# A selective scan turned round: states on the partitions instead of channels, in a four-block kernel on one core

## The reference

```
def _L1_attn_ref(x, ...):                     # Mamba: d_inner = 256, n_state = 16, CHUNK = 32
    ...
    delta = jax.nn.softplus(dlt @ W_dt.T + b_dt)          # per token and channel
    A = -jnp.exp(A_log)                                   # per channel and state
    dA = jnp.exp(jnp.einsum('bld,dn->bldn', delta, A))
    dBu = jnp.einsum('bld,bln,bld->bldn', delta, Bm, u)
    ...
    def step(carry, inp):
        a, bu, c = inp
        carry = a * carry + bu
        y = jnp.einsum('bkdn,bkn->bkd', carry, c)         # sum over the 16 states
        return (carry, y)
    ...                                                   # started anew every 32 tokens
    y = y * jax.nn.silu(res)
    return y @ W_out.T + b_out
```

## Time and profile before

| what | us |
|---|---|
| median of 3 runs | 1242.27 (1234.53 to 1244.73) |
| the profiled execution | 1238.27 |
| its span | 1236.5 |
| PE busy, of the span | 1003.6 |
| DVE busy | 819.9 |
| POOL busy | 725.4 |
| ACT busy | 656.3 |

### The profile page before, as it was taken

One profiled execution on the slowest core, in us unless ns is written; L12 is line 12 of the kernel. 1 busy time (PEld: TensorE's weight loads), 2 busy tenths in 40 slices (PEclk: granted clock), 3 DMA queues, 4 the chain that ended last, 5 costly groups with the idle time before them and its releaser, 6 DMA issues.

```text
span 1236.5 us, 11304 instructions
## 1 busy us (share of the span) xinstructions
PE 1003.6 (81%) x3604; PEld 500.5 (40%) x3604; DVE 819.9 (66%) x1473; ACT 656.3 (53%) x1020; POOL 725.4 (59%) x572
## 2 busy tenths in 40 slices
PE   0455889789989999879998999879887976977785
PEld 0233535335535544444544535434333332332231
DVE  1412231585766786578879886898688789789751
ACT  1133465665675667756686656665624643553231
POOL 0012133757667747675877677776866786787422
PEclk9866788788878899889899988989978987897996
DMA  4000200453434524254552554545554665576420
GB/s 110 0 9 1 77 1 21 160 194 113 179 104 153 206 113 153 68 206 152 205 181 104 212 192 150 180 173 176 205 186 190 205 225 179 198 254 213 144 103 17
DMA packets 55715, 176.60 MB, mean 143 GB/s; under 512 B 7332, under 2 KB 17896, under 8 KB 51560
## 3 DMA queue, kind: packets, MB, share of 16 engines
q1 hardware_dynamic: 55656, 175.89, 41.0%
HBM read 172.99 MB, written 2.88 MB: 142 GB/s over the span
## 4 chain that ended last, share of the span: by engine, by line
PE 50%; DVE 19%; POOL 12%; ACT 10%; issue 4%; DMA 3%; SPq 2%; POOLq 0%; DVEq 0%; ACTq 0%
PE yp L1366 12%; DVE hs L899 5%; PE mp L1261 4%; PE pp L1298 4%; POOL dbu L638 4%; PE fp L1165 4%; PE mp L1271 4%; PE fp L1173 3%; DMA bcast<-held 3%; PE fp L1179 3%; DVE hs L906 2%; ACT L928 2%; PE mp L1277 2%; SPq L379 2%; PE pp L1230 2%
## 5 line engine op out<-in xcount | busy, mean ns | idle before, releaser
L638 POOL TENSOR_TENSOR dbu<-du,bcast 128x1024 f32<-128x1024 f32 x128 | 341.0, 2667 | 142.4 <-DMA bcast<-held 74.4
L899 DVE TENSOR_TENSOR_SCAN hs<-dA,dbu 128x512 f32<-128x512 f32 x256 | 300.4, 1206 | 58.7 <-POOL dbu L638 18.1
L1366 PE MATMUL yp<-hs,ident 128*128 128x512 f32 x512 | 294.9, 709 | 38.6 <-DVE hs L906 26.7
L1121 ACT ACTIVATE dA<-delta,mA 128x496 f32<-128x496 f32 x256 | 169.4, 672 | 145.2 <-DVE hs L899 142.0
L1366 PEld LDWEIGHTS yp<-hs,ident 128*128 128x128 f32 x512 | 107.0, 224 | 179.1 <-issue 110.7
L906 DVE TENSOR_TENSOR hs<-hs,bcast 128x1024 f32<-128x1024 f32 x96 | 156.9, 1634 | 2.9
L836 DVE SCALAR_TENSOR_TENSOR he<-mp,vectors,he 128x512 f32<-128x512 f32 x128 | 89.8, 741 | 40.9 <-PE mp L1261 40.4
L928 ACT ACT_TABLE_LOAD x77 | 98.8, 1283 | 1.4
L1261 PE MATMUL mp<-cont,w_e 64*128 64x512 f32 x256 | 88.8, 697 | 10.6 <-DVE he L836 8.8
L622 POOL TENSOR_TENSOR hs<-hs,bcast 128x1024 f32<-128x1024 f32 x32 | 75.2, 2349 | 17.1 <-DVE hs L899 17.0
L1165 PE MATMUL fp<-f_zT,w 128*128 128x512 f32 x128 | 72.0, 689 | 2.2 <-ACT f_zT L948 2.2
(11 more groups left out here) (212 smaller groups left out, 1536.1 us busy)
## 6 DMA issues: line engine op xcount, KB each, us to landing
bcast<-held SPq DMA_DIRECT2D x128, 1024.0 KB, 5.3
he<-gates SPq DMA_DIRECT2D x32, 1024.0 KB, 6.7
xin<-L_attn_x SPq DMA_DIRECT2D x8, 256.0 KB, 2.9
out<-xo SPq DMA_DIRECT2D x8, 256.0 KB, 2.3
held<-bc SPq DMA_DIRECT2D x8, 64.0 KB, 3.5
he<-conv_wT SPq DMA_DIRECT2D x1, 384.0 KB
w<-w1T SPq DMA_DIRECT2D x1, 256.0 KB
he<-w2T SPq DMA_DIRECT2D x1, 256.0 KB
```

The source lines that it names most:

```text
L638: pool.tensor_tensor(out=dbu[:, j % 2, :].rearrange("p (r t) -> p r t", r=2), in0=d, in1=b_n, op=ALU.mult).then_inc(dbu_r.sem, 1)
L899: dve.tensor_tensor_scan(out=hs[:, j % 2, half], data0=dA[:, half], data1=dbu[:, j % 2, half], initial=0.0, op0=ALU.mult, op1=ALU.add).the ...
L1121: act.activation(out=dst, in_=src, func=ACT.Exp, scale=mA[:, c, n:n + 1]).then_inc(dA_r.sem, 1)
L1366: last = pe.matmul(yp[:, :], lhsT=ident[:, :], rhs=hs[:, j % 2, r * SEQ:(r + 1) * SEQ], start=(k == 0 and r == 0), stop=(k == PAIRS - 1 an ...
```

## The change

A step now has 8 channels (LANES) with all their 16 states on the 128 partitions, and two such groups of 8 channels as the halves of the free dimension. There are still 16 steps an image, two exponentials, two scans and two products a step, of the same sizes.

- B and C no longer change from step to step: `bnc` (state on the partition) is filled once an image by two DMAs of 256 KB.
- delta and du must reach all 16 states of a channel. They go out to DRAM by 16 DMAs of 64 KB an image (`to_rows`) and come back spread, two DMAs of 512 KB a step: `ds` (3 buffers) for the exponential and `hs` (6 buffers) for the product with B.
- The product with B, the scan and the product with C are all made in place in `hs`; `dbu` is gone. The scan no longer waits for the sum; the refill of an `hs` buffer does.
- `delta` and `du` are single buffers now, which wait for the transfers out of the image before.
- The sum over states: a matrix `place` (128 x 32) adds the 16 states of 8 channels and puts them on one of four places of 8 rows. The four groups of two neighbouring steps go to four column tiles of 32 rows of `yp`, so two steps make one piece of PE's thread, with four matmuls.
- ORDER has new tables for all five engines.

```diff
-SLOTS = 3
+LANES = P // STATES
+GROUPS = P // LANES
+PAIRS = GROUPS // 2
+COLS = 32
+PLACES = COLS // LANES
+SLOTS = 6
+DELTAS = 3
...
+            def to_rows(i, rows, src, out_done):
...
+                for c in range(IC):
+                    for j in range(P // COLS):
+                        sp.dma_start(rows[i % 2, c, j // 2, :, j % 2, :], src[j * COLS:(j + 1) * COLS, c, :]
+                                     ).then_inc(out_done.sem, 16)
+
+            def step_rows(rows, i, c, k):
+                src = rows[i % 2, c, k % 2, k // 2 * LANES:(k // 2 + 1) * LANES, :, :]
+                return src.rearrange("(a c) r t -> a c (r t)", a=1).broadcast_to([STATES, LANES, 2 * SEQ])
...
+                    sp.wait_ge(delta_r.sem, delta_r.at(i, 1))
+                    to_rows(i, delta_rows, delta, delta_out)
+                    yield True
+                    sp.wait_ge(du_r.sem, du_r.at(i, 1))
+                    to_rows(i, du_rows, du, du_out)
+                    yield True
+                    sp.wait_ge(bc_out.sem, bc_out.at(i, 16))
+                    if i >= 2:
+                        sp.wait_ge(sum_ps.sem, sum_ps.at(i - 1, 0))
+                    for which in range(2):
+                        src = held[i % 2, which, :, :].rearrange("n (a t) -> n a t", a=1)
+                        sp.dma_start(bnc[:, i % 2, which, :], src.broadcast_to([STATES, LANES, SEQ])
+                                     ).then_inc(bnc_in.sem, 16)
...
-                            src = held[i % 2, :, 2 * k:2 * k + 2, :].rearrange("(a s) r t -> a s (r t)", a=1)
-                            sp.dma_start(bcast[:, j % SLOTS, :, :], src.broadcast_to([P, 2, 2 * SEQ])
-                                         ).then_inc(bc_in[j % SLOTS], 16)
+                            if j >= DELTAS:
+                                sp.wait_ge(dA_r.sem, 2 * (j - DELTAS + 1))
+                            sp.dma_start(ds[:, j % DELTAS, :], step_rows(delta_rows, i, c, k)
+                                         ).then_inc(ds_in[j % DELTAS], 16)
+                            if j % STEPS == 0:
+                                sp.wait_ge(du_out.sem, du_out.at(i + 1, 0))
                             if j >= SLOTS:
...
+                                sp.wait_ge(sum_ps.sem, (j - SLOTS) // 2 + 1)
+                            sp.dma_start(hs[:, j % SLOTS, :], step_rows(du_rows, i, c, k)
+                                         ).then_inc(du_in[j % SLOTS], 16)
...
+            def times(j, which):
+                h = hs[:, j % SLOTS, :].rearrange("p (r t) -> p r t", r=2)
+                return pool.tensor_tensor(out=h, in0=h, in1=both(bnc[:, j // STEPS % 2, which, :]), op=ALU.mult)
...
+                if i >= 1:
+                    dve.wait_ge(delta_out.sem, delta_out.at(i, 0))
+                    dve.wait_ge(du_r.sem, du_r.at(i - 1, 1))
...
                                     dve.wait_ge(dbu_r.sem, j + 1)
-                                    if j >= 2:
-                                        dve.wait_ge(sum_ps.sem, j - 2 + 1)
...
+                for ic in range(BATCH * IC):
+                    for k in range(PLACES):
+                        yield True
...
+                        for j in (ic * PAIRS + 2 * k, ic * PAIRS + 2 * k + 1):
                             by_gpsimd, by_pool, by_dve = with_c(j)
...
                             for r in range(2):
-                                last = pe.matmul(yp[:, :], lhsT=ident[:, :], rhs=hs[:, j % 2, r * SEQ:(r + 1) * SEQ],
-                                                 start=(k == 0 and r == 0), stop=(k == PAIRS - 1 and r == 1))
-                            last.then_inc(sum_ps.sem, 1)
+                                at = COLS * (2 * (j % 2) + r)
+                                last = pe.matmul(yp[at:at + COLS, :], lhsT=place[:, k, :],
+                                                 rhs=hs[:, j % SLOTS, r * SEQ:(r + 1) * SEQ],
+                                                 start=(k == 0), stop=(k == PLACES - 1))
+                        last.then_inc(sum_ps.sem, 1)
```

192 lines of the change are left out of this document (95 added, 97 removed).

## The result

The changed kernel takes **1314.3 us** (median of 4 runs, 1309.2 to 1316.6) against 1241.9 for the kernel before on the same chip: a ratio of 1.058, 95% interval [1.053, 1.063]. It is 5.8% slower where I forecast 1171 us. The profiled execution took 1316.3 us, with a span of 1314.6.

What follows compares the result with a forecast made beforehand. PE was taken to set the pace from 228 to 890 us, with DVE the busiest after the change. 1238.3 - 68 - 20 + 16 + 1 = 1167, plus 4.0 for the timed runs, gave 1171 us, range 1130 to 1205.

Steps and rivals of the forecast that it cites:

- The sums over the states: PE's sums on four column tiles: a pair of steps takes 1.1 us, 0.30 of the old 3.70.
- Tiles in turn: Rival on PE's sums: four tiles run one after the other, no gain, 1258 to 1283 us; chance 0.08.
- The first and the second stretch: Scans from 228 to 890 us and 890 to 1168 us: PE's relief gains 68 us and 20 us.
- The clock: PE's granted clock from 228 to 890 us falls from 0.90 to about 0.85, making 477 us of work 505.
- my 1167: Whole kernel: the summed forecast in us against the profiled execution, before 4.0 us were added for the timed runs.
- They move the same megabyte a step: Step transfers on SP's queue: 256 instead of 128, and 144 more for rows and bnc, at no cost.
- The way through DRAM: From du to the first product with B: 10.4 us more an image, half counted at images 4 to 6, 16 us lost.
- exposed everywhere: Rival: the way through DRAM is exposed at every image, 67 us more, 1238 us; chance 0.06.
- The new tables: Engines' order: no cost of its own; for images 4 to 6 delta is made only as the scan before ends.
- The refill: hs buffers on SP's queue: six give slack instead of three; the rival that refill waits for PE had chance 0.03.

Runs made afterwards that it cites:

- wide_sums: Changed kernel with the sums over states as 128-column matmuls one after another instead of four column tiles: 1367.9 us, 1.106 of the kernel before.
- before_few_sums: Kernel before, under its own tables, with PE's sums cut to 28% of their columns: 1231.3 us, 0.993 of the kernel before.
- both: Changed kernel with the edits of one_row and image_0 together: 1259.5 us, 1.016 of the kernel before.
- no_transfers: Kernel of both with step transfers left out after the first steps that fill ds and hs: 1256.0 us, 1.015 of the kernel before.
- one_row: Changed kernel with each step transfer reading one 4 KB row for all 128 partitions instead of eight rows: 1292.9 us, 1.044 of the kernel before.
- before_form: Kernel before with bcast filled by two 512 KB transfers a step, written in the form 16 x 8: 1277.3 us, 1.028 of the kernel before.
- image_0: Changed kernel with only image 0's delta and du rows sent to DRAM, all images reading those: 1281.5 us, 1.035 of the kernel before.
- old_order: Changed kernel under the order tables of the kernel before, fitted to its pieces: 1354.3 us, 1.092 of the kernel before.

## Why the prediction was wrong, point by point

- **The sums over the states: right.** A pair takes 1.06 us at the full clock, forecast 1.1; no gap for the change of tiles shows. The group takes 139.0 us, forecast 80 to 100: the lower clock held for many of its rows, and nearly half of the steps ran as half pairs, which cost as much as whole ones. Tiles in turn, the rival, did not happen, and wide_sums says what they would have cost.
- **The first and the second stretch: the step that failed.** I took the share at which an engine had been seen, 91.5% or 85%, as what the stretch must reach again once PE's work is less, and gained 68 + 20 us. Under the old tables the relief alone gives 9 (before_few_sums), 8 of them in the scans, with PE idle for 18% of the first stretch and its end 2 us earlier. In both and no_transfers, which have the relief, the new tables and the new waits but not the price of the transfers, the scans are 11 to 12 us shorter than before, where I had 88. That is 77 of the 149 us between my 1167 and the 1316.3 of the profiled execution. It does not say that relief is worth 9 everywhere: in the changed kernel, under its own tables, the tiles are worth 54 (wide_sums). What the relief would give the old layout under tables made for it, no run tried. I read a busy PE as the pace of the stretch; PE's busy time was itself stretched by the clock, and with less of it the other engines went no faster.
- **The clock.** 0.83 in the first stretch is within what I gave, with 0.85 taken. Behind it, where I let it stand, it fell from 0.86 to 0.71. PE was forecast at 798 us and has 951.8; its other matmuls alone grew by 104. But relief and lower clock together are a gain in the changed kernel (wide_sums has the higher clock and is slower); the clock's own part in the miss stays open.
- **"They move the same megabyte a step", at no cost: failed.** The pattern holds the engines 1.29 times as long (54.4% of 1314.6 us against 43.2% of 1288.0); `hs` and `ds` land in 7.6 and 6.4 us, where I took 3.7. It costs 21 us (one_row), 40 in the old kernel (before_form). I had read size from the rows and not form, and the mean share of 0.46 to 0.58 as slack; in the last scan it now is 1.03.
- **The way through DRAM: right mechanism, too small.** 15.6 and 16.2 us (images 6 and 0) and not 10.4; 33 us in all (image_0) against 16, and 12 to 14 more at image 0, to which I gave zero since PE was the bound. The rival "exposed everywhere" had the sign of it.
- **The new tables.** I cost them at nothing. They put image 0's `delta` 10 to 12 us later, and are better for this scan all the same than the old ones (old_order is 40 us slower).
- **The refill.** Six buffers of `hs` give no slack: the issue stands behind the wait for `ds`'s three. It costs nothing either, since with four nothing changed.

The ledger of spans: 1236.5 + 27.3 ahead of the scans - 11.1 of relief, new tables and new waits together (937.4 to 926.3) + 59.0 of pattern and way (926.3 to 985.3, singly 25.5 and 38.6) + 2.9 behind = 1314.6. Each part has its run, but for the split of the 27.3 into tables and way, which rests on the rows of `delta`, and for the split of the 11.1, which is open: with the wide sums the changed kernel's scans take 1036.5, with the old tables 1030.5. Open is which chain of waits holds the old scans at 930 us; only that neither PE's sums nor half of DVE's products with C are most of it was shown.

## What to carry to other kernels

An engine busy for 91% of a stretch need not set its pace. Before a redesign that relieves it, leave that work out of the old kernel and time it: one run of before_few_sums would have shown 9 us where this forecast had 88. Such a run holds for the order and the waits that it was made under, and a relief can be worth more in another layout, as wide_sums showed. Price a transfer by its access pattern and not by its bytes, by a run in which the old transfer is written in the new form. And where a layout sends data through DRAM, cost the way at the first image and at each one after it, with every issue that stands ahead in the queue.

## What the runs showed of the hardware

- A transfer of 512 KB from one row of 4 KB to 128 partitions written as 16 x 8 instead of 128, with the same packets, raised the share of the DMA queue from 40.3 to 52.0% and the landing from 4.7 to 6.1 us. Written as 8 x 16 the whole kernel became 21% slower than as 16 x 8, with 8 packets fewer for each transfer and a DMA share of 0.51 at 210 GB/s in the last scan, against 1.03 at 248.
- Float32 matmuls in four column tiles of 32 overlap: eight rows of 512 columns in 1.06 us, against 3.70 for eight 128-wide ones. Four rows on two of the tiles take as long as eight on four, 1.92 and 1.94 us at the lower clock.
- With PE's sums cut by 182 us the granted clock fell from 0.90 to 0.84 and from 0.86 to 0.74, and the rest of PE's work took 80 us more.
- With the DMA engines full in parts of the scans, transfers that a fourth buffer let go out earlier landed later by 3.2 and 3.0 us (6.4 to 9.6, 7.6 to 10.6), and the time stayed (1312.1 against 1314.3).
